# When the SyncE queue asks for the weights of the expert after the next

## What is computed

```
logits = flat @ gate_w + gate_b                  # 4096 tokens, 8 experts
topv, topi = top_k(logits, 2)                    # each token goes to 2 experts
routing[t, topi] = softmax(topv)
for each expert e:                               # w1: 256x1024, w2: 1024x256, f32
    h   = gelu(flat @ w1[e] + b1[e])
    out = h @ w2[e] + b2[e]
    acc = acc + out * routing[:, e]
x = x + layernorm(acc)
```

## Time and profile before

| | us |
|---|---|
| median of 3 timed executions | 688.99 |
| their lowest and highest | 685.15, 689.6 |
| the profiled execution | 692.22 |
| span of its record | 690.4 |
| PE busy in the span | 562.9 (82%) |

### The profile page before, as it was taken

One profiled execution on the slowest core, in us unless ns is written; L12 is line 12 of the kernel. 1 busy time (PEld: TensorE's weight loads), 2 busy tenths in 40 slices (PEclk: granted clock), 3 DMA queues, 4 the chain that ended last, 5 costly groups with the idle time before them and its releaser, 6 DMA issues.

```text
span 690.4 us, 14876 instructions
## 1 busy us (share of the span) xinstructions
PE 562.9 (82%) x4170; PEld 507.8 (74%) x4175; DVE 425.9 (62%) x1446; ACT 366.7 (53%) x821; POOL 184.4 (27%) x153
## 2 busy tenths in 40 slices
PE   2768756766855798999999999989989999999920
PEld 1536344344345598999999999989989999999910
DVE  4958764936885675555545556558567754454547
ACT  3364632734733544464646456667569554553651
POOL 2000071071072266232322222312213231312210
PEclk9958977967977989999999999999999999999975
DMA  8910020091021176332323235355365232322567
GB/s 226 381 35 0 1 100 23 0 334 48 1 100 40 65 180 210 56 46 46 46 46 46 46 46 170 48 153 168 46 167 159 40 55 38 54 38 47 163 154 245
DMA packets 51848, 66.73 MB, mean 97 GB/s; under 512 B 4870, under 2 KB 45292, under 8 KB 51692
## 3 DMA queue, kind: packets, MB, share of 16 engines
q1 hardware_dynamic: 37804, 47.87, 22.0%
q0 software_dynamic: 14016, 18.56, 15.7%
HBM read 38.26 MB, written 28.74 MB: 97 GB/s over the span
## 4 chain that ended last, share of the span: by engine, by line
PE 61%; DVE 11%; ACT 9%; issue 7%; another core or an unknown queue 7%; DMA 3%; DVEq 1%; ACTq 0%; POOLq 0%; POOL 0%
PE pY L1527 24%; PE pL L1515 23%; PE pP L722 3%; DMA sum_y<-y,dest 2%; PE pP L823 2%; PE pS L739 2%; PE pX L439 2%; DVE z L1652 2%; ACT xn L569 1%; ACT z L1666 1%; PE pT L707 1%; ACT xrow L636 1%; PE pS L788 1%; ACT h L1450 1%
## 5 line engine op out<-in xcount | busy, mean ns | idle before, releaser
L1450 ACT ACTIVATE h<-pL,b_now 128x256 f32<-128x256 f32 x272 | 112.3, 464 | 152.5 <-PE pL L1515 146.0
L517 POOL DMA_INDIRECT sum_y<-y,dest x70 | 113.6, 1623 | 286.0 <-DVE y L1571 261.0
L1527 PE MATMUL pY<-w_hi,h_lo 128*128 128x256 f32 x544 | 154.9, 285 | 4.8 <-DVE h_lo L1544 4.5
L1515 PE MATMUL pL<-xeT_hi,w_lo 128*128 128x256 f32 x544 | 151.7, 279 | 6.3 <-issue 5.7
L1527 PE MATMUL pY<-w_hi,h_hi 128*128 128x256 f32 x544 | 151.7, 279 | 0.0
L1527 PE MATMUL pY<-w_lo,h_hi 128*128 128x256 f32 x544 | 151.5, 279 | 0.0
L1515 PE MATMUL pL<-xeT_lo,w_hi 128*128 128x256 f32 x544 | 151.1, 278 | 0.0
L1515 PE MATMUL pL<-xeT_hi,w_hi 128*128 128x256 f32 x544 | 150.9, 277 | 0.0
L1544 DVE TENSOR_TENSOR h_lo<-h,h_hi 128x512 fp32r<-128x512 f32 x136 | 92.8, 691 | 93.6 <-ACT h_hi L1456 92.6
L1515 PEld LDWEIGHTS pL<-xeT_hi,w_lo 128*128 128x128 f32 x544 | 102.0, 187 | 7.6 <-issue 6.9
L1527 PEld LDWEIGHTS pY<-w_hi,h_lo 128*128 128x128 f32 x544 | 102.9, 189 | 6.0 <-DVE h_lo L1544 5.4
(11 more groups left out here) (266 smaller groups left out, 844.5 us busy)
## 6 DMA issues: line engine op xcount, KB each, us to landing
w_stage<-w SPq DMA_DIRECT2D x16, 1024.0 KB
xt<-sorted_x SPq DMA_DIRECT2D x38, 260.0 KB
sum_y<-fill SPq DMA_DIRECT2D x1, 4352.0 KB, 19.6
w_stage<-sum_y SPq DMA_DIRECT2D x8, 512.0 KB, 7.8
out<-z SPq DMA_DIRECT2D x8, 512.0 KB, 3.0
x_all<-x SPq DMA_DIRECT2D x3, 1024.0 KB, 8.3
sorted_x<-fill SPq DMA_DIRECT2D x8, 260.0 KB
sum_y<-y,dest POOLq DMA_INDIRECT x70
```

The source lines that it names most:

```text
L517: pool.indirect_dma_start(out=sum_y, out_offset=bass.IndirectOffsetOnAxis(ap=to[:, i:i + 1], axis=0), in_=rows[:, i, :], in_offset=None, c ...
L1450: a = act.activation(h[:, c, :], pL[:, bk, i * TM:(i + 1) * TM], ACT.Gelu, bias=b1_now[par][:, c:c + 1])
L1515: mm = pe.matmul(pL[:, bk, i * TM:(i + 1) * TM], w[:, 0, col], x[:, k, :], start=(k == 0 and w is lo), stop=(k == KC - 1 and x is xeT_lo))
L1527: mm = pe.matmul(pY[:, i, 0:D], s[:, c, rows], w[:, 1, c * D:(c + 1) * D], start=(c == 0 and s is h_lo), stop=(c == FC - 1 and w is lo))
```

## The change

SP no longer asks for weights at the beginning of a place that has three tiles or more. There it does its first two tiles (the loads of rows that stand behind them), then asks, and goes on with the third. For a place with fewer than three tiles it asks at the beginning, as before. The waits ahead of the two requests stay the same. The table `steer` gets one more entry. No other engine's program is touched.

```diff
-TAB = 64 + TPE
+TAB = 65 + TPE
...
-        def over_tiles(eng, start, first, none, tile, roomy=False, between=None):
+        def over_tiles(eng, start, first, none, tile, roomy=False, between=None, ask=None):
...
+                if ask:
+                    if not type(e) is int:
+                        with eng.If(n < 3):
+                            ask(e, par)
+                    with eng.If(n >= 1):
+                        tile(e, who, par, base)
+                        with eng.If(n >= 2):
+                            tile(e, who, par, base + 1)
+                            with eng.If(n >= 3):
+                                ask(e, par)
+                                with eng.Fori(0, TPE // 4) as u:
+                                    four = 4 * u + 2
+                                    with eng.If(n > four):
+                                        with eng.Fori(0, 4) as v:
+                                            with eng.If(n > four + v):
+                                                tile(e, who, par, base + four + v)
+                            eng.sem_inc(passed, 1)
+                    return
...
-            def start(e, pair, par, base):
+            def ask_weights(e, par):
                 if type(e) is not int:
...
-            over_tiles(sp, start, first, None, tile, between=between)
+            over_tiles(sp, None, first, None, tile, between=between, ask=ask_weights)
```

## The result

| | before | after |
|---|---|---|
| median of 20 executions each, taken in turn on one chip | 689.47 | 691.91 |
| ratio, 95% interval | | 1.004, 1.0025 to 1.0054 |
| the profiled execution | 692.22 | 691.89 |
| span of its record | 690.4 | 690.1 |

I forecast 688.0, 1.0 us less than before; it became 2.4 us more. The time lies inside the range. From `over_tiles` on, the changed kernel's lines are numbered 18 higher (`pL` 1533, `pY` 1545, `h_lo` 1562, `dest` 1571, `y` 1581 and 1589, the load of rows 1394).

A forecast was written before the change was run, and what follows sets the result against it. It took PE's two layers to bound the kernel, with reachable gains only where PE waits. Terms -3.5 + 0 + 2.3 + 0.2 = -1.0 us took 688.99 to 688.0 us, range 684.0 to 693.0.

The forecast's parts named there:

- What is late next is ACT's fourth bank: Tile 3: bank moves 3.3 us earlier with POOL, to 272.6; gain 3.5 us, bounds 0 and 4.65.
- places 1 and 3: Last tiles of both places: moved weights slow the scatters ahead of DVE's taking of rows; loss 2.3 us, bounds 0 and 4.0.
- rival 3: Moved scatters cost nothing and the whole stall in tiles 2 and 3 goes: 684.3 us; chance 0.12.
- Queues: DMA engines take turns between queues, so overlapping weights slow scatters; served first come, first served, places 1 and 3 cost near 0.
- Beside tiles 4 and 5: Place 0's weights now arrive there and slow tile 3's scatters, which cover absorbs: cost 0, bounds 0 and 3.2 us.
- SP itself: SP's added comparison per place and level of branches are covered by its waits ahead of loads: cost 0.
- PE's pace: Place 0: the fast matmul pace may set in one tile later; cost 0.2 us.
- rival 2: PE keeps the slow pace through place 0, tiles 4 to 15 costing 4.9 us: 692.7 us; chance 0.08.

The follow-up runs named there:

- p0_only: Against the kernel before, only place 0's weight request moves behind its second tile; places 1 and 3 ask at their beginning: 690.3 us, ratio 1.0052.
- hold_y: Kernel before, but from place 1 on SP asks for weights only once the scatters ahead have landed: ratios 0.9962, 0.9976 and 0.9997 on three chips.
- after_third: The changed kernel, unaltered, timed once more against the kernel before: 689.84 us beside 686.85, ratio 1.0048.
- p13_only: Against the kernel before, only the requests of places 1 and 3 move; place 0 asks at its beginning: 686.47 us, ratio 0.9987.
- p13_again: Repeat against the kernel before with only the requests of places 1 and 3 moved: 687.63 us beside 686.85, ratio 1.0019.
- after_spread: The changed kernel with POOL's row sends spread otherwise, five instead of eight in a row behind tile 1's scatters: 687.6 us, ratio 1.0013 to the kernel before.
- pause_again: The changed kernel with one more POOL wait ahead of its last five sends, breaking the row of eight: 687.79 us beside 686.85 for the kernel before, ratio 1.001.
- after: The changed kernel itself, as profiled first, against the kernel before: 691.91 us, ratio 1.004.

## Why the prediction was wrong

*The failed step* is "What is late next is ACT's fourth bank ... I move it with POOL". I had seen that the bank's signal was held up by 7.03 us inside POOL's row of sends and ended with it, and treated that as one late signal with a place. What the runs showed in its place: on chip A the row of sends holds up what PE issues or signals, wherever it lies, and the bank was one case of it. With POOL's wait gone, the row is eight long without a break, and its last third lies over tile 3's first layer, where PE is on the chain with nothing to cover it: 5.2 us for four matmuls, then 3.6 us at the low clock. The fourth bank, forecast for 272.6, was taken at 273.87, which is 275.9 counted from the start of the loops as in the record of before: it had not moved at all. So the stall did leave (POOL released at 258.9, rows in time, no wait for `xt`, all as forecast), and one of the same size took its place: tiles 2 and 3 took 30.2, 30.7 and 28.2 us in the records with the change of place 0, and 28.1, 26.3, 27.6 and 27.0 in those without (the two groups barely separate). Gain forecast 3.5; measured by those means -2.5 (27.2 against 29.7). Shown: place 0's part carries the loss on chip A, the loss is not there on chip C, which has no hold-ups, and with a break of 2.9 to 4.0 us in the row PE does not crawl (five records of five, against three crawls in three without one). Not shown: why signals are late in four of these five all the same, and whether it is PE's instruction supply or its semaphores that the sends hold up.

*Mis-sized: places 1 and 3.* Loss forecast 2.3 (0 to 4.0), measured none: both places together took 70.9 to 71.7 us in the kernels that move their requests, 72.4 before, and 71.3 in p0_only, which moves neither, so that even the 1 us of difference is PE's pace (hold_y, which moves neither behind its second tile, took 72.5 on chip B and 70.9 on chip C). The weights left 1.6 us behind the rows, a scatter took 2.5 to 2.7 us more rather than 4.1, and that is under the 2.9 us that I had named as covered. That was rival 3's half of the truth, and my text had named the test.

*Queues.* The scatters were slowed wherever they met weights, though the weights had been asked for 3 us ahead of them: in place 0 the one of 283.40 was released at 289.9, 6.5 us. The record shows the core's traffic at 297 to 385 GB/s from 282 to 288 us and 87 GB/s from 288 to 290: scatter and weights ended at about the same time. Service in turns (the Trainium skill, DMA: Bandwidth & Descriptors, Queues, rings and completion order) allows that, but so does first come, first served, since 2 MB took some 8 us here, longer than my sentence "gone well before" assumed. No run here decides between them, and the cost was 0 either way.

*Beside tiles 4 and 5*: cost 0, right; the cover of 0.2 to 1.1 us held, since the scatter took 6.5 us and not 8.

*SP itself*: forecast 0 for the added branches. In fact from the load of rows to the next place's request SP took 6.7 us instead of 5.5 (502.19 to 508.86; p0_only 6.4), and that load had itself gone out 1.6 us later (its tags stood behind the slower scatter). The 2.8 us kept the weights clear of place 3's last scatter. In this record and in after_third places 4 to 6 then took 1.5 and 1.6 us less; but in p13_only, p13_again and after_spread, where the same scatter was alone too (3.8 us), they took only 0.2 to 0.6 less. The next scatter, beside place 5's weights, took 7.0 and 7.1 us in the first two and 8.1 to 8.5 in the other three, with the same distance between the issues; why is open. hold_y keeps both scatters clear and got 36.4 to 36.7 us there on all three chips.

*PE's pace*: forecast +0.2, rival 2 +4.9. It did wander between 113 and 118 ns a matmul: +1.0 us in tiles 4 to 15, about -1 in places 1 and 3, +1.1 in the rest. Rival 2's trigger did not hold: without the wait at 278.2 the fast pace came back all the same a tile or two later. The rest is 0.3 to 1.2 us longer than in the record of before in every other kernel on chip A but pause_again, and 1.0 longer on chip C in the kernel before too, so it is no effect of the change.

*The sum* of the record's stretches is +1.6 us (407.8 to 409.4), the timed difference +2.4. The loops start anywhere from 245.7 to 251.6 us in the records of chip A, so the remaining 0.8 can't be placed; it stays open. (The two whole records differ by -0.3 us, since the one of the changed kernel reached its loops 2.0 us earlier, ahead of anything that the change touches.)

No version beats both kernels on every chip: hold_y is ahead of the kernel before on B and C (0.9962, 0.9976; the changed kernel was not timed on B, and against its 0.999 on C the intervals overlap) and is level with the kernel before on A.

## What to carry to other kernels

A wait that is taken out of a sending engine makes its sends denser. Before booking the gain, look at what the same engine's dense stretches do to the others elsewhere in the trace: here three rows of sixteen sends in the first half had signals late by up to 8 us already. A gap in which one engine waits may be what the others live on.

What a moved transfer collides with matters more than when it starts: price a moved request at each meeting by the margin of the one that waits, and test whether that margin exceeds the slowing before charging it.

And a stall seen in one record may belong to the chip: the one that this change was to remove is not there in the kernel before on chip C, and on chip B the nearest kernel with a trace (hold_y) waits 1.1 us at that place.

## What the runs showed of the hardware

- On chip A, in all three records with eight back-to-back indirect sends of POOL (0.96 us each, 0.30 between) behind tile 1's scatters, PE's issue is held up (gaps of 0.34 to 1.15 us between single matmuls in after and p0_only) and signals from PE come late (waits of 5.8 to 7.9 us), up to 1.8 us past the last send in after. With a break of 2.9 to 4.0 us behind the third send there was no crawl in five records, but in four of them a signal to ACT was still late. On chips B and C eight in a row did neither.
- The kernel before takes 687 us on the one and 654 to 655 on the others, with loops of 407.8 against 402.9 us, of which tiles 2 and 3 make 4.6; the rest of the difference lies ahead of the loops (they start at 251.6 against 217.5).
- A scatter beside 2 MB of weights took 6.4 to 6.6 us when asked 3 us behind them, 7.0 to 8.9 when within about 2 us of them either way, 9.4 in hold_y on chip B (222.54 to 231.9, weights at 224.86), and 3.8 to 4.2 with no weights beside it.
